# Five more edge columns summed by one-hot matmuls in the sheaf layer of a four-layer graph network (75 of 125, not 70)

## The reference, cut to what matters

```python
xs, xd = (x[src], x[dst])                      # 400000 x 16 each
h = relu(concat([a, b]) @ W1.T + b1); h @ W2.T + b2     # "reflection", for (xs, xd) and (xd, xs)
F_s, F_d = householder(reflection(xs, xd)), householder(reflection(xd, xs))
L_sd = -einsum('eki,ekj->eij', F_s, F_d)
coef = deg_inv_sqrt[src] * deg_inv_sqrt[dst]
msg_s = coef[:, None] * einsum('eij,ej->ei', L_sd, xd)
msg_d = coef[:, None] * einsum('eji,ej->ei', L_sd, xs)
out = x - zeros_like(x).at[src].add(msg_s) - zeros_like(x).at[dst].add(msg_d)
```

## Time and profile before

| | |
|---|---|
| median of three runs | 24477.58 us |
| profiled execution: its time, its span | 24502.01 us, 24500.3 us |
| sheaf layer's passes over chunks (first gather to last tile) | 7882 to 15159 us |
| busy over the whole span: GpSimd, TensorE, VectorE, ScalarE | 74%, 65%, 52%, 8% |
| granted TensorE clock, mean over the span | 0.795 |

### The profile page before, as it was taken

The page is one execution under the profiler, slowest core; times in us unless marked ns, Lnnn a source line. Parts: engine busy times, 40 slices in busy tenths (PEclk is TensorE's granted clock), DMA queues, the critical chain, the costliest instruction groups (busy, mean ns, idle before and its releaser), DMA issues. The chain is left out here.

```text
span 24500.3 us, 265915 instructions
## 1 busy us (share of the span) xinstructions
PE 15809.6 (65%) x89068; PEld 10242.0 (42%) x89500; DVE 12705.3 (52%) x23081; ACT 1881.4 (8%) x4697; POOL 18130.0 (74%) x15859
## 2 busy tenths in 40 slices
PE   0688862887881788888888886699999860000005
PEld 0344431444440455555555554577777640000004
DVE  2688872554542556655556654455555423333331
ACT  0000000000000111111111110111111110000001
POOL 5777765777775788888888885788888727777775
PEclk9888875888885788888888888799999875555557
DMA  2222220111111111122111121233333226666663
GB/s 92 50 60 61 65 53 16 43 44 39 44 39 22 31 31 31 31 41 32 31 31 31 31 37 32 49 48 51 51 51 47 33 85 205 206 206 205 204 204 113
DMA packets 1982980, 1698.45 MB, mean 69 GB/s; under 512 B 791143, under 2 KB 1742950, under 8 KB 1964470
## 3 DMA queue, kind: packets, MB, share of 16 engines
q0 software_dynamic: 928000, 564.95, 15.1%
q10 hardware_dynamic: 821300, 579.22, 7.5%
q1 hardware_dynamic: 232322, 536.71, 6.5%
HBM read 996.31 MB, written 683.38 MB: 69 GB/s over the span
## 5 line engine op out<-in xcount | busy, mean ns | idle before, releaser
L1405 POOL DMA_INDIRECT acc<-column_sums,sum_rows x3375 | 5683.2, 1684 | 1192.9 <-issue 1141.3
L1347 PE MATMUL node_sums<-placed_row,lane_values 128*128 128x392 bf16 x34500 | 6176.9, 339 | 523.2 <-DVE placed_row L1335 523.0
L803 POOL DMA_INDIRECT gathered<-gat_table,src_index x4906 | 4865.7, 992 | 1525.2 <-issue 1500.4
L1347 PEld LDWEIGHTS node_sums<-placed_row,lane_values 128*128 128x128 bf16 x34500 | 3459.1, 102 | 2958.3 <-DVE placed_row L1335 549.0
L1626 POOL DMA_INDIRECT gathered<-sheaf_table,src_index x3125 | 3389.7, 1085 | 958.9 <-issue 947.0
L2352 POOL DMA_INDIRECT gathered<-message_table,src_index x3125 | 3055.7, 978 | 986.2 <-issue 952.1
L587 PE MATMUL transposed<-ident,last_rows 128*128 128x128 f32 (+3 forms) x5 | 2.2, 441 | 4064.1 <-DVE sums L619 4064.1
L1335 DVE TENSOR_SCALAR placed_row<-iota_rows_f,src_row 128x1568 bf16<-128x1568 f16 x2875 | 1795.4, 649 | 1122.0 <-PE node_sums L1347 1092.8
L1010 PE MATMUL lanes_ps<-S,table_parts 128*128 128x512 bf16 x8676 | 2050.7, 396 | 308.4 <-DVE S L875 298.1
L1010 PE MATMUL lanes_ps<-code_onehot,table_parts 128*128 128x512 bf16 x8676 | 2046.3, 395 | 297.3 <-DVE code_onehot L875 287.1
L587 PEld LDWEIGHTS transposed<-ident,last_rows 128*128 128x128 f32 (+3 forms) x5 | 0.7, 148 | 4066.1 <-DVE sums L619 4066.1
(11 more groups left out here) (446 smaller groups left out, 19260.9 us busy)
## 6 DMA issues: line engine op xcount, KB each, us to landing
message_rows<-gathered ACTq DMA_DIRECT2D x250, 1600.0 KB, 10.5
src_rows<-src_rows SPq DMA_DIRECT2D x200, 640.0 KB
src_rows<-src_rows SPq DMA_DIRECT2D x125, 960.0 KB
code_rows<-src_code_rows SPq DMA_DIRECT2D x336, 256.0 KB, 3.2
gat_rows<-scanned ACTq DMA_DIRECT2D x25, 3375.0 KB
gathered<-gat_table,src_index POOLq DMA_INDIRECT x4906
acc<-column_sums,sum_rows POOLq DMA_INDIRECT x3375
gat_rows<-scanned ACTq DMA_DIRECT2D x25, 2125.0 KB, 7.0
```

The costliest lines, as they stand in the source:

```text
L803: g.indirect_dma_start(G[b][:, j, :], None, tab, bass.IndirectOffsetOnAxis(ap=IX[b][:, j:j + 1], axis=0)).then_inc(s_g[b], 16)
L1347: last = pe.matmul(o.acc[:, m, 0:Q8 // 4], lane, o.OW[r][:, m * (Q8 // 4):(m + 1) * (Q8 // 4)], start=first(k, 1) and i == 0 and part == 0 ...
L1405: g.indirect_dma_start(self.acc[i], bass.IndirectOffsetOnAxis(ap=o.IXS[b][:, j:j + 1], axis=0), o.SV[b][:, j, :], None, compute_op=ALU.add ...
```

## The change

`MT` grows from 70 to 75. So 75 tiles (15 groups) are summed in PSUM and 50 columns, not 55, are scatter-added. `opens` and the number of lane buffers are shifted by one more group, so that the buffers stay five and groups 8 to 12 are still the ones opened at once. The extra group goes ahead of the reflection: the old last group's place now opens group 13 (`MT // ACCS - 2`), then come the five one-hots of tiles 45 to 49, then group 14's lane values.

```diff
-MT = 70
+MT = 75
...
-            self.tile_buffers(c, o, MT, [...], (MT - SG * ACCS) // ACCS - 1,
+            self.tile_buffers(c, o, MT, [...], (MT - SG * ACCS) // ACCS - 2,
...
-            opens = [range(q, q + 1) for q in range(SG)] + [range(SG, MT // ACCS - 1)]
+            opens = [range(q, q + 1) for q in range(SG)] + [range(SG, MT // ACCS - 2)]
...
                         w(v.tensor_scalar(n2[:], n2[:], 1e-24, None, ALU.max))
                         if not first(k, 1):
+                            self.lane_values(v, o, k - 1, 1 - b, MT // ACCS - 2, parts)
+                            late(ACCS)
                             self.lane_values(v, o, k - 1, 1 - b, MT // ACCS - 1, parts)
                         w(v.reciprocal(n2[:], n2[:]))
```

More of the change, by code:

```diff
@@ L1561, in sheaf_edges @@
             flat = Q[:].rearrange("p c f -> p (c f)")
-            self.tile_buffers(c, o, MT, [sb(f"placed_row{i}", [P, Q8], BF16)[:] for i in range(ACCS)], (MT - SG * ACCS) // ACCS - 1,
+            self.tile_buffers(c, o, MT, [sb(f"placed_row{i}", [P, Q8], BF16)[:] for i in range(ACCS)], (MT - SG * ACCS) // ACCS - 2,
                               V[:].rearrange("p c f -> p (c f)")[:, 0:Q8])
```

## The result

The changed kernel took 24560.3 us in the median of seven runs (24546.94 to 24599.1). The kernel before took 24489.57 us beside it (24475.53 to 24502.31). The ratio is 1.0032, with a 95% interval of 1.0020 to 1.0044: slower, by about 70 to 80 us. The profiled execution took 24583.53 us (span 24581.7), 82 us more than that of before. All of it lies in the sheaf layer: from its first gather to the first copy of the finished sums it takes 7362.1 us, not 7276.7 (+85.4). The rest of the program differs by 4 us the other way.

The account below looks back on a forecast made before the run. GpSimd was taken to bound at 284.2 us a chunk; the VectorE/TensorE loop, 273.2 + 15.5 = 288.7 us, would take over. 22 x 4.5 + 2 x 15.5 + 10 = +140 us, forecast 24617 us, own range 24565 to 24650, 8 in 10 24540 to 24665.

Parts of the forecast that it names:

- TensorE's slow start: Sixty matmuls of tiles 45 to 49, slowed after TensorE's idle: +2.2 us over full-clock time, range 1.2 to 2.9.
- What bounds before: Sheaf layer: GpSimd issues without a break and sets the 284.2 us chunk; the VectorE/TensorE loop has 11.0 us of slack.
- Part 1: GpSimd: five scatter-adds fewer a chunk save 10.0 us, giving a pass of 274.3 us.
- Part 2: Ahead of the reflection: VectorE waits for tiles 45 to 49 before group 14; reciprocal +15.1 us (14.1 to 15.9).
- Part 3: From the reciprocal on: nothing given back, and wider operands add 0.4 us, together +15.5 us a chunk on the loop.
- Part 4: Chunk's border: TensorE's late loop return against faster first tiles, together set to 0, range -2 to +1 us a chunk.
- The sum: Whole kernel: 22 chunks at +4.5 us, two at +15.5 us and 10 us for the last tiles, +140 us.
- rival A: Border gives back most, reciprocal late by 14.1 us: +1.5 us a chunk, +68 us, 24546; chance 0.15.
- B: Rival: VectorE does not stand still for group 14; only 6.0 us of work counts, -88 us, 24390; chance 0.07.
- the very best: All of GpSimd's 10 us come through, with a loop longer by only 1 us: -206 us, 24272.
- C: Rival: border costs 1 us, clock late (+2.9), another TensorE idle; 18.5 us on the loop, +212, 24690; chance 0.10.
- the return of TensorE's loop: Every second chunk: if as long as VectorE's 3.33 us, TensorE's first tile there comes 1.5 us late.

Follow-up runs that it names:

- e3: Kernel before with one group of five scatter-adds of each sheaf chunk not issued (70 tiles, 50 scatters): 24245.8 us, ratio 0.9898 to the kernel before.
- e6: Changed kernel with one group of five scatter-adds of each sheaf chunk not issued (75 tiles, 45 scatters): 24572.3 us, ratio 1.0031 to the kernel before.
- e2: Changed kernel with a sixth lane buffer in the output buffer, used by group 9, so group 14 follows group 8: 24260.3 us, ratio 0.9902 to the kernel before.
- e4: Changed kernel with MT = 70, so the kernel before's 70 tiles and 55 scatter-adds in the changed order: 24472.6 us, ratio 0.9987 to the kernel before.
- e7: Kernel before with MT = 65, so 65 tiles and 60 scatter-adds: 24687.3 us, ratio 1.0071 to the kernel before.

## Why the prediction was right in kind and too large

The sign, the mechanism and the place were right; the size was 24617 - 24478 = 139 us forecast, against 71 us between the medians and 82 us between the two profiled executions. Two terms were too large and both erred the same way: the delay of the reciprocal by 1.2 us a chunk, because of TensorE's slow start in it, and the chunk's border by 1.6. On a loop of which 11 us are slack, 2.7 us too much in 15.5 made the added period 4.5 us, where 1.8 came.

- **What bounds before.** Right. GpSimd's pass set the period (e3: -10.6 us a chunk for five scatters; 10.0 forecast), and the slack of VectorE and TensorE was 11 us. The 16.6 us of VectorE's own wait would have misled: with it, no loss would have been forecast.
- **Part 1, the gain of 10 us on GpSimd.** Right, and worth nothing behind the longer loop (e6).
- **Part 2, VectorE's stall.** Right in kind (8.6 us in the mean behind five one-hots; 10 forecast). The term that was too large is TensorE's slow start: +2.2 us was taken for the 1.2 GHz level after the idle. The forecast took it from what followed idles of 3.7, 5.2 and 9.6 us, and from the granted clock of 0.59 within the last of these; the idle here is 2.93 us, and the clock within it was 1.00 in chunks 8 and 9. The slow start was +1.7 us in half of the chunks and 0 in the others, 0.8 in the mean. The reciprocal came late by 13.9 us, below the range of 14.1 to 15.9.
- **Part 3, nothing given back.** The late one-hots and TensorE's idle stand as forecast. The wider operands and what else lies behind the reciprocal cost 0.6 us, for 0.4.
- **Part 4, the chunk's border.** Set to 0, measured at -1.6 us, within the -2 to +1 kept. TensorE no longer idles 9 us ahead of a chunk. Its first 60 matmuls took 11.54 us in chunk 8 in place of 13.00, at a granted clock of 0.87 for 0.77, and over chunks 2 to 23 10.71 us in the mean in place of 12.36.
- **The sum.** In place of the 15.5 us a chunk forecast for the loop came 12.85. Behind a slack of 11.1 us that left 1.8 us a chunk, for 4.5: 40 us in 22 chunks where 99 stood, and chunk starts 286 us apart, not 288 to 290. Counted between first lane values, chunk 1 cost 16.6 us and the last chunk with its tiles 24.9 us (15.5 and 25.6 forecast), and chunk 0 came 3.5 us later. 40.5 + 16.6 + 24.9 + 3.5 = 85.5 us, which is the +85.4 of the result but for rounding.
- **The rivals.** What came is rival A, to which 0.15 had been given: an early reciprocal and a border that gives back, a loop of 286.0 us where A had 285.7 and the forecast 288.7, and a time 71 us above the median where A had 68. The forecast's own range, 24565 to 24650, just missed it; the range for 8 in 10, 24540 to 24665, holds it. B's condition, a free buffer, is not that of the changed kernel, but it can be made true (e2), and then 24260 us came where B had 24390, next to the 24272 named as the very best. Its 6.0 us of work proved to be 1.9, since most of it fits into the wait for tile 44. C did not come: the border gave time back, the slow start was never over 1.7 us, and only 0.6 us was lost behind the reciprocal.

The reading of the return of TensorE's loop is not settled. A wait "issue" ahead of the transposes of 8.5 us in 10 times stands in the waits of after, 0.85 us in the mean and 1.2 at most; 1.5 us had been allowed for it. VectorE's 3.3 us came again: 32.8 us in 10 times. The Trainium skill (Advanced Engine Details and Errata, Control Flow Timing) gives a compare-and-branch about 108 ns. The trace does not speak against that: in the kernel before, VectorE's branch itself is recorded with 0.063 us in each of the ten returns from 8400 to 14700 us, and its next record follows 2.7 to 3.0 us later. So the prediction set two things against each other, the instruction and the whole return of the loop. No run changed the loop, so what fills the time behind the branch is open.

## What to carry to other kernels

When work moves from the engine that sets the period to a loop with slack, first find that slack at the last wait that ties one turn of the loop to the next, not at the engine's longest wait. Then ask of every added buffer user which earlier user must be finished, and what stands between the two: here five one-hots, a group of lane values and a wait for the tiles just made delayed the reciprocal by 13.9 us, and the same work without the wait (e2) by 0.6. A buffer that another stage writes only later in the same pass can serve in the meantime.

## What the runs showed of the hardware

GpSimd's pass is no sum of fixed durations. A gather takes 0.947 us in the median, but one that met VectorE's L1803, an addition with two inputs of 4000 elements (the prediction calls it a product), took 4.5 us. The same 125 gathers had a mean of 1091 ns in the kernel before, 1065 in e4 and 1045 in e7. The traces show a part of what changed: between 8500 and 14300 us, 20 gathers of the kernel before started while L1803 ran, and took 4.47 us each; in e7 it was 1 gather, and 20 scatter-adds, which took 3.92 us each. Five scatter-adds were worth 10.6 us a chunk in e3 and 6.8 us in e7, and e4, which issues the same transfers as the kernel before, had a pass at least 2 us shorter.

TensorE's granted clock did not always follow the same idle either: behind 2.93 us without a matmul, 60 of them took 11.80 us in chunk 8 (granted clock 0.85) and 10.12 us in chunk 9 (1.00).
